# Attention scan over both batches at once, packed small matmuls, rewritten weight setup of the FFN

## The reference

```
x  = x + ga * RWKV6(layernorm(x) * (1 + ca) + sa)
x  = x + gb * FFN(layernorm(x) * (1 + cb) + sb)
RWKV6: xxx = h + sx*maa_x; m = tanh(xxx @ tm_w1)        # 512 -> 5*32
       x_f = h + sx*(maa_f + m_f @ tm_w2[f])            # f = w,k,v,r,g
       r,k,v = x_f @ W; g = silu(x_g @ Wg)              # 512 -> 512
       w = exp(-exp(decay + tanh(x_w @ td_w1) @ td_w2)) # 512 -> 64 -> 512
       per head (16 heads of 32), token by token:
         y = r (S + u * k v^T);  S = w * S + k v^T
       out = (groupnorm(y) * g) @ Wo
FFN:   fp4lin(silu(fp4lin(h, w_gate)) * fp4lin(h, w_up), w_down)   # 512 -> 1408 -> 512
       fp4lin quantises both operands in blocks of 16 to an FP4 grid
```

## Time and profile before

| | |
|---|---|
| median of 3 runs | 4452.12 us (4444.54 to 4455.94) |
| profiled execution | 4452.27 us, span 4450.3 us |
| PE busy | 3871.5 us (87%) |
| VectorE busy | 3532.5 us (79%) |
| ScalarE, POOL busy | 1551.0 us, 1144.8 us |
| mean granted TensorE clock | 0.928 |

### The profile page before, as it was taken

How to read it: one execution, slowest core, us unless ns; L and a number is a source line. 1 busy time by engine, 2 the same in 40 slices (tenths; PEclk the granted TensorE clock), 3 DMA queues, 4 the chain that set the end, 5 groups by cost and what they waited for, 6 DMA issues and landing times. The chain is left out here.

```text
span 4450.3 us, 152657 instructions
## 1 busy us (share of the span) xinstructions
PE 3871.5 (87%) x64712; PEld 2617.5 (59%) x64712; DVE 3532.5 (79%) x7737; ACT 1551.0 (35%) x2811; POOL 1144.8 (26%) x736
## 2 busy tenths in 40 slices
PE   4889888898898988988989871479999999999999
PEld 3767767676676776776767650235454555545454
DVE  4777767777777776777777757879999999999997
ACT  2434334343343332433434311333333333333333
POOL 1121211211112112111121112533333333333332
PEclk7999989999999998999999985689999999999999
DMA  3000000000000000000000002001011011011010
GB/s 108 12 22 27 22 27 17 22 26 22 23 22 22 27 17 22 26 22 27 17 22 26 13 22 83 29 29 36 30 36 37 29 37 37 30 37 36 30 36 29
DMA packets 73003, 133.17 MB, mean 30 GB/s; under 512 B 12705, under 2 KB 13473, under 8 KB 72290
## 3 DMA queue, kind: packets, MB, share of 16 engines
q1 hardware_dynamic: 72290, 123.00, 8.5%
HBM read 89.43 MB, written 33.55 MB: 28 GB/s over the span
## 5 line engine op out<-in xcount | busy, mean ns | idle before, releaser
L712 POOL TENSOR_TENSOR xf<-xf,hT 128x1024 f32<-128x1024 f32 x128 | 310.0, 2422 | 1189.6 <-DVE xf L762 1189.6
L878 DVE COPY_PREDICATED Am<-pick,banks 128x64 f32<-128x64 uint8 (+2 forms) x1792 | 460.6, 257 | 125.3 <-DVE Am L878 8.6
L1563 PE MATMUL fbank<-dT,hqT 128*128 128x512 f16 x2112 | 489.5, 380 | 19.8 <-ACT hqT L1480 19.7
L1551 PE MATMUL fbank<-gT,xqT 128*128 128x464 f16 (+1 forms) x2304 | 491.0, 363 | 11.2 <-issue 6.4
L1551 PE MATMUL fbank<-uT,xqT 128*128 128x464 f16 (+1 forms) x2304 | 488.0, 361 | 1.8 <-issue 1.8
L723 POOL TENSOR_TENSOR yrs<-yvar,neg_half 128x32 f32<-128x32 f32 x32 | 174.0, 5438 | 894.6 <-DVE yvar L907 894.6
L1551 PEld LDWEIGHTS fbank<-gT,xqT 128*128 128x128 f16 x2304 | 225.6, 98 | 248.2 <-issue 12.5
L1551 PEld LDWEIGHTS fbank<-uT,xqT 128*128 128x128 f16 x2304 | 225.1, 98 | 234.4 <-issue 4.8
L1491 ACT ACTIVATE sil<-fbank,und 128x464 f32<-128x464 f32 (+1 forms) x192 | 124.1, 647 | 659.0 <-PE fbank L1551 658.8
L762 DVE SCALAR_TENSOR_TENSOR xf<-banks,col_maa,sx 128x256 f32<-128x256 f32 x640 | 265.2, 477 | 90.9 <-PE banks L462 90.1
L1563 PEld LDWEIGHTS fbank<-dT,hqT 128*128 128x128 f16 x2112 | 196.5, 98 | 235.2 <-ACT hqT L1480 30.2
(11 more groups left out here) (230 smaller groups left out, 8523.4 us busy)
## 6 DMA issues: line engine op xcount, KB each, us to landing
x_tok<-in_L_attn_x SPq DMA_DIRECT2D x32, 512.0 KB, 3.9
xres<-in_L_attn_x SPq DMA_DIRECT2D x32, 512.0 KB, 3.5
x_after_attention<-xres SPq DMA_DIRECT2D x32, 512.0 KB, 3.5
xl<-x_after_attention SPq DMA_DIRECT2D x64, 256.0 KB, 2.7
xr<-x_after_attention SPq DMA_DIRECT2D x64, 256.0 KB, 2.7
out<-xr SPq DMA_DIRECT2D x64, 256.0 KB, 2.1
raw_g<-in_L_wmod SPq DMA_DIRECT2D x3, 1024.0 KB, 5.1
raw_g<-in_L_ffn_w_gate SPq DMA_DIRECT2D x1, 2816.0 KB, 10.2
```

The costliest lines, as they stand in the source:

```text
L712: nc.gpsimd.tensor_tensor(xf[:, j % NXF].rearrange("p g b t -> p (g b) t"), xf[:, j % NXF].rearrange("p g b t -> p (g b) t"), hT[:, :, :, ...
L878: nc.vector.copy_predicated(dst, mask, src).then_inc((done or A_step).sem, 1)
L1551: last = nc.tensor.matmul(GU[2 * pair + t][:, 0:w], xqT[:, u, a, g, :], W[:, b_, g, lo_:hi_], start=(k == 0), stop=(k == 3 * G - 1))
L1563: last = nc.tensor.matmul(DN[1 - u][:], hqT[:, a, kk, :], dT[:, b_, kk, :], start=(first and kk == 0), stop=(end and kk == KF - 1))
```

## The change

1. **The scan takes both batches in one step.** A chunk has four steps `q`. `pe_scores(q)` has 128 matmul calls into one set of banks (two for scores, one for the middle part), and waits for `dve_A(q-1)`. `dve_A(q)` has the same ten operations with twice the elements. `pe_y(q)` has 64 calls into two y banks, one for each batch.
2. **Other fill order** on TensorE, ScalarE and VectorE.
3. **Small products are packed.** `tm1`'s last 32 columns run as four 32-column groups with 64 tokens each, `td1` as two 64-column groups, one for each batch, `td2` as two 64-row groups. The activations behind them cover more partitions and fewer columns. `act_stack` copies the last mix in 16 pieces instead of four. The bias of `td2` moves into `dve_ww`, now four operations with a bias column.
4. **FFN setup rewritten.** The gate weights are loaded first and each matrix gets its scales just before its tiles. A tile has three VectorE operations (scale, and two with a grid that ScalarE computes), POOL makes high and low parts directly (VectorE makes the high part of two tiles), the modulation products are cut into four parts each, and PSUM copies are merged.

```diff
-        PROJ, SC, YB = bank[2:4], bank[4:6], bank[7]
-        XB = (bank[0], bank[6])
-        XT = (bank[1], bank[6])
+        PROJ, SC, YB = bank[2:4], bank[4:6], bank[6:8]
+        XB = bank[0]
+        XT = (bank[1], bank[0])
...
+        def pe_scores(pe, c, q):
...
+            else:
+                settled_after(pe, mod_done, (A_done, c, q))
+            t = slice(32 * q, 32 * q + 32)
+            for b in range(B):
+                for g in range(G):
+                    X = (g * B + b) * Q + q
+                    for d in HEADS:
+                        nc.tensor.matmul(SC[b][d, g * P:g * P + NS], kvar[d, 0, g, b, t], rcol[d, X, 0:M1], start=True, stop=True)
...
+            for k in range(G):
+                for d, rows in enumerate(HEADS):
+                    last = nc.tensor.matmul(SMALL[rows, BT:BT + QT], w_tm1[:, k, P:P + A_RANK], xxx[:, k].rearrange("p b t -> p (b t)")[:, QT * d:QT * (d + 1)],
+                                            start=(k == 0), stop=(k == G - 1))
...
+                for b in range(B):
+                    last = nc.tensor.matmul(SMALL[HALVES[b], 0:TC], w_td1[:, k, :], xf[:, 0, k, b], start=(k == 0), stop=(k == G - 1))
...
+                for b in range(B):
+                    last = nc.tensor.matmul(PROJ[b][:, g * TC:(g + 1) * TC], w_td2[HALVES[b], g * P:(g + 1) * P], u1[HALVES[b]], start=True, stop=True)
...
-            for n in range(1, 8):
-                if do_w:
-                    pe_scores(pe, c, n)
-                    if n <= 2:
-                        pe_g(pe, c, n - 1, do_p)
-                    pe_y(pe, c, n - 1)
-                if n == 3 and do_p:
-                    pe_td1(pe, i)
-                if n <= 5 and do_p:
-                    pe_delta(pe, i, n - 1)
-                if n == 4 and do_f:
-                    pe_wo(pe, f, 0, do_p, do_w)
-                if n == 6 and do_p:
-                    pe_td2(pe, i)
-                if n == 6 and do_f:
-                    pe_wo(pe, f, 1, do_p, do_w)
+            (guards left out) pe_g(0); pe_delta(0); pe_scores(1); pe_y(0); pe_g(1); pe_delta(1);
+            pe_scores(2); pe_td1; pe_y(1); pe_delta(2); pe_wo(0); pe_delta(3); pe_scores(3);
+            pe_y(2); pe_delta(4); pe_wo(1); pe_y(3); pe_td2; pe_x(i + 1);
+            pe_proj(1), both halves; pe_proj(2); pe_tm1(i + 1); pe_proj(3); pe_scores(i, 0)
...
+                    if f < 4:
+                        last = nc.scalar.activation(m_stack[rows, j, :], m_part[part % 2][HEADS[f], 0, :], ACT.Copy)
+                    else:
+                        for d in range(4):
+                            last = nc.scalar.activation(m_stack[rows, j, QT * d:QT * (d + 1)], m_part[part % 2][HEADS[d], 1, 0:QT], ACT.Copy)
...
-            nc.vector.tensor_scalar(flat4(wexp), banks[:, 2:4].rearrange("p s n -> p (s n)"), 80.0, None, ALU.min).then_inc(ww_done.sem, 1)
+            for g in range(G):
+                last = nc.vector.tensor_scalar(wexp[:, g], banks[:, 2:4, g * TC:(g + 1) * TC], col_decay[:, g:g + 1], 80.0, ALU.add, ALU.min)
+            last.then_inc(ww_done.sem, 1)
...
             # FFN setup, VectorE, each tile n
+                        V.scalar_tensor_tensor(a, m, GRID, a, ALU.max, ALU.add).then_inc(s_done.sem, 1)
...
+                        V.scalar_tensor_tensor(q16[:, p, 0:w], m, GRID, a, ALU.max, ALU.subtract).then_inc(q_done.sem, 1)
...
             # FFN setup, POOL, each tile n
+                        if t < 2 or r % 2 == 0:
+                            nc.gpsimd.tensor_tensor(view(hi[:, p, 0:w]), view(q16[:, p, 0:w]), spread(s_high), ALU.mult).then_inc(hi_done.sem, 1)
+                        nc.gpsimd.tensor_tensor(view(lo[:, p, 0:w]), view(q16[:, p, 0:w]), spread(s_low), ALU.mult).then_inc(lo_done.sem, 1)
```

More of the change, by code:

```diff
@@ L391, in sp_body @@
                 sp.dma_start(x1[:, tok(f), :].rearrange("b t n -> t b n"), xres[:]).then_inc(x1_stored.sem, 16)
[L394 to L397, removed]
+        def pe_scores(pe, c, q):
+            if q == 0:
                 settled_after(pe, mod_done, (der, c), (ru_done, c), (m1_done, c), (k_done, c), (derk, c, 2))
[L399 to L411, removed]
@@ L412, in pe_scores @@
+            if q == 0:
                 settled_after(pe, mod_done, (vT_done, c), (kT_done, c))
-            for g in range(G):
-                for d in HEADS:
-                    last = nc.tensor.matmul(sc[d, G * NS + g * K:G * NS + (g + 1) * K], kT[d, g, b, q, :], v_s[d, g, b, q, :], start=True, stop=True)
+            for b in range(B):
+                for g in range(G):
+                    for d in HEADS:
+                        last = nc.tensor.matmul(SC[b][d, g * P + NS:g * P + NS + K], kT[d, g, b, q, :], v_s[d, g, b, q, :], start=True, stop=True)
@@ L416, in pe_scores, with pe_y @@
             last.then_inc(score_done.sem, 1)
[L418 to L423, removed]
-            else:
[L425 to L433, removed]
+        def pe_y(pe, c, q):
+            if q == 0:
+                settled_after(pe, mod_done, (A_done, c, q + 1), (yT_done, c - 1))
+            else:
+                settled_after(pe, mod_done, (A_done, c, q + 1))
+            for b in range(B):
+                for g in range(G):
+                    X = (g * B + b) * Q + q
+                    for d in HEADS:
+                        nc.tensor.matmul(YB[b][d, g * P + 32 * q:g * P + 32 * q + 32], v_s[d, g, b, q, :], Am[d, q % 2, b, g, :], start=True, stop=False)
+                    for d in HEADS:
+                        last = nc.tensor.matmul(YB[b][d, g * P + 32 * q:g * P + 32 * q + 32], state[d, b, q, g, :], r32[d, X, :], start=False, stop=True)
@@ new lines, in _ @@
+                    for n in range(len(items)):
+                        if first(n):
+                            for m in range(lead(n)):
+                                grid(n + m)
+                        if ahead(n):
+                            grid(n + lead(n))
+                        if not first(n):
+                            evacuate(n - 1)
+                        if n + 1 == len(items) or first(n + 1):
+                            evacuate(n)
+                        if n in ROW_AT:
+                            m = ROW_AT.index(n)
+                            act.wait_ge(modf_done.sem, 2 * (m + 1))
+                            for b in range(B):
+                                if m == 0:
+                                    last = nc.scalar.activation(row_sb[:, b], mod_bank[0][b][:], ACT.Copy)
+                                else:
+                                    last = nc.scalar.activation(row_cb[:, b], mod_bank[1][b][:], ACT.Identity, bias=ones[:])
+                            last.then_inc(row_done.sem, 1)
@@ L1223, in _ @@
[L1223 to L1226 removed]
+                        link(V.tensor_reduce(sc[:, t], flat, AX_X, ALU.max, apply_absolute_value=True))
+                        link(V.tensor_scalar(sc[:, t], sc[:, t], 1.0 / 6.0, 1e-12, ALU.mult, ALU.max))
```

447 lines of the change are left out of this document (239 added, 208 removed).

## The result

| | before | after |
|---|---|---|
| median | 4453.94 us (4444.54 to 4462.76) | 4487.34 us (4468.66 to 4494.37) |
| profiled span | 4450.3 us | 4487.4 us |
| attention, to the first DMA of the setup | 2687.7 us | 2762.4 us |
| FFN setup | 206.9 us | 169.4 us |
| FFN loop | 1555.7 us | 1555.6 us |

The ratio is 1.0067, 95% interval 1.0042 to 1.0092: slower by 33 us (0.7%), where 4450 and no change were forecast. The attention lost 74.7 us, the setup gave back 37.5.

A forecast was written before the change was run, and what follows sets the result against it. The prediction took TensorE to bound the kernel, its scan runs going at the pace of instruction arrival. Loop +50 and setup -50 on 4452.3 us gave 4452, stated as 4450 us, range 4350 to 4530.

The forecast's parts named there:

- TensorE work -2.8: Packed td1, td2 and tm1's narrow half on TensorE save 2.8 us a chunk (bounds +0.3, -3.3).
- Instruction arrival +3.8: On TensorE, closer scan instructions wait more for instruction packets: stalls go from 7.6 to 11.4 us a chunk.
- the 788 run: Before's longest run of scan instructions on TensorE: 788 took 9.79 us for an estimated 5.9 of work, losing 3.9.
- Clock +0.8: More stalls lower TensorE's clock on the projections behind them: 0.8 us a chunk lost (bounds 0 and +2.8).
- Waits -0.2: TensorE's waits for ww grow 0.7 us a chunk, those at kT shrink 0.9 (bounds -1, +2).
- They cover it: Work between score steps on TensorE hides VectorE's A; for A(0), 3.7 + 0.7 us against 3.7.
- R3: Rival: the single set of score banks binds, scores waiting for A; +3 us a chunk more, 4545 us, chance 0.08.
- Setup -50: The rewritten FFN setup falls from 206.9 to 157 us, 50 less (bounds -30 and -67).
- Loop +50: The attention loop's terms sum to +1.6 us a chunk, x 31 = +50 us (bounds -5 to +9 a chunk).
- VectorE's 7.8 us a chunk, worth nothing: The scan merge frees 7.8 us a chunk on VectorE, off the path with 20 us free, so no time won.

The follow-up runs named there:

- e11: The kernel after with packing undone (tm1, td1, td2, tanh, stacking and ww as before), merge, order and new setup kept: 1.0113 times before.
- e2: The kernel after with the merge undone (eight steps, two sets of score banks, before's order), packing and new setup kept: 0.9814 times before.
- e1: The attention of the kernel before with the rewritten FFN setup alone: 0.9916 times before.
- e4: The kernel after with each 16-column score matmul issued twice, 512 instructions more a chunk: 1.0503 times before.
- e13: The kernel after with useless 128x128 matmuls on constants added between the two batches of scores(1) to (3): 1.0054 times before.
- e5: The kernel after with TensorE work spread between scan matmuls and scores(1) to (3) halved by batch, projection pieces between the halves: 0.9670 times before.
- e7: The kernel after with four of the seven predicated copies of every A(q) on VectorE left out: 0.9914 times before.
- e10: The kernel after with four more, repeated, predicated copies in every A(q) on VectorE: 1.0211 times before.

## Why the prediction was wrong

- **The step that failed: "TensorE work -2.8", taken as time won.** In their own rows the packed products save 2.8, but e11 without them is only 0.2 to 0.5% slower than after (0.4 to 0.7 us a chunk), within its interval. I priced the packed products by their work alone and left out that they are 80 instructions more a chunk, though the pace of arrival stood in my own sum. Of the 2.8 us, 1.2 come back as busy time of other groups, 1.2 as arrival and 0.7 as waits for ww and A. In before's order (e2) packing gave 1.5.
- **What hid its size: the rest of the sum missed the other way.** Arrival, clock and waits were +4.4 a chunk. e11, which has the merge and no packing, is 2.1 us a chunk over before by the period and 2.8 by its ratio against e1. That +50 stood as near to +74.7 as it did is luck, as far as two opposite misses go.
- **Instruction arrival +3.8: right as idle time.** The merge and its order without packing show 7.5 to 11.4, +3.9; with packing 12.6. The mechanism, a pace of arrival in dense runs, is borne out from both sides by e4 and e13. The unit was coarse: 256 instructions in 3.7 to 3.8 us rather than 245 in 3.04, which fits halved runs (e5) still stalling. The loss of 3.9 us in the 788 run was also too high: TensorE is recorded busy there for 6.98 us and not 5.9; matching the sum to the measured 7.6 evened that out.
- **Clock +0.8:** the clock fell to 0.88, where I had only said at or under 0.93. Its price stands in groups such as the gate projection behind `scores(1)` and y, whose mean (the second number) was 407 ns before:

```profile
L509 PE MATMUL banks<-xf,w_g 128*128 128x256 f32 x864 | 216.6, 407 | 4.7 <-ACT gu L661 3.1 <-issue 1.6
```

```profile
L509 PE MATMUL banks<-xf,w_g 128*128 128x256 f32 x832 | 263.9, 485 | 18.5 <-issue 18.3
```

  Sixteen a group, two groups a chunk, 78 ns each: 2.5 us a chunk, three times the term. Busy time as a whole fell all the same, by 1.2 us a chunk even in e11, whose work is before's; ends of short matmuls are modelled in the profile, and that balance stays open.
- **Waits -0.2:** ww cost 0.8 as said. "They cover it" for A was wrong in part: A(0) needs 3.8 of 4.4 us, and e7 and e10 show that A's length counts. R3 as I priced it (+3 a chunk) did not happen.
- **Setup -50:** -37.5, 12 us short. The tile was 3.52 us instead of 2.85, from VectorE and POOL slowing each other. Along the timeline the narrow tiles of both matrices with their first links took 72.7 us against 62.3 in the sum (+10), the four wide tiles with theirs 36.5 against 29.0 (+7.5; VectorE's operation of 1408 columns 4.00 us beside POOL and 1.62 alone). The start to the first maximum was 12.4 and not 10.3 (+2); scales were 5 us cheaper (36.1 against 40.8) and the tail 3. I had taken each engine's duration from rows in which the other did something else.
- **Loop +50:** +74.7. Loop and setup missed by 25 and 12 us in the same direction, so the forecast of no change became +33 measured. The range held it. The lower bounds of the parts sum to -3.9 a chunk, not to the -5 given.
- **VectorE's 7.8 us a chunk, worth nothing:** its busy time fell to 53.2 us as summed, and after is no faster for it. But the merge made a single A longer (2.8 to 3.85 us), and e7 and e10 show that this length costs; the sum had it at nothing.

## What to carry to other kernels

Where the profile shows idle called "issue" in front of tiny matmuls, count instructions between the stalls. Work put between them was free here (6.0 us a chunk), and work taken out was worth at most part of its busy time, so spread long matmuls among the short ones before shrinking them. And take a duration from a row in which the engine's neighbours do what they will do after the change.

## What the runs showed of the hardware

- 6.0 us of useless TensorE work a chunk made the kernel no slower (ratio 1.0054 beside 1.0089) and raised the granted clock from 0.88 to 0.93.
- VectorE's two-tensor operation of 512 columns takes 0.68 us alone and 1.54 beside a POOL product of 1.44; beside one of 1.00 it takes 1.10. POOL's product of 512 columns takes 1.05 us beside a reduction on VectorE and 1.44 to 1.50 beside two-tensor operations.
- Where TensorE has little work between stalls, 256 of its instructions take 3.7 to 3.8 us.
- 64-column `td1` in two column groups: 1.94 to 1.09 us; tm1's 32 columns in four: about 1.9 to 0.65 us. The Trainium skill's "TensorEngine Tiling (Array Packing)" (Theoretical Speedup) allows 2x and 4x; these are 1.8x and 2.9x.
